# Where a pair mask is made in a graph-net and expert kernel: moved from the expert block to the first row stage

## The reference

```python
x = x + L0_gnn(layernorm(x), src, dst, edge_attr_20, edge_weight, edge_attr_4, ...)   # message passing
x = x + L0_ffn(layernorm(x), gamma, beta, Wd, splines, Wu, scale)                    # one of 64 experts a row
x = x + L1_gnn(layernorm(x), edge_index, node_vec1, ...)                             # 4 blocks of attention + MLP
x = x + L1_ffn(layernorm(x), w_gate, w_up, w_down)                                   # gated feed-forward
# attention of L1_gnn, per head
scores = einsum('ehd,ehd->eh', q[src], k[dst])
attn = exp(scores - smax[src]) / segment_sum(exp(...), src)
out = segment_sum(attn[:, :, None] * v[dst], src)
```

## Time and profile before

| what | value |
|---|---|
| median of 3 runs | 2948.11 us |
| the profiled execution's own time | 2946.58 us |
| its span, first to last instruction | 2944.9 us |
| mean granted TensorE clock | 0.933 |
| busy: PE, PEld, DVE, ACT, POOL | 86%, 74%, 64%, 47%, 40% |
| moved by DMA | 220.43 MB |

### The profile page before, as it was taken

One profiled execution on the slowest core, in us unless ns is written; L12 is line 12 of the kernel. 1 busy time (PEld: TensorE's weight loads), 2 busy tenths in 40 slices (PEclk: granted clock), 3 DMA queues, 4 the chain that ended last, 5 costly groups with the idle time before them and its releaser, 6 DMA issues. The chain is left out here.

```text
span 2944.9 us, 38864 instructions
## 1 busy us (share of the span) xinstructions
PE 2521.8 (86%) x13585; PEld 2166.0 (74%) x13585; DVE 1889.2 (64%) x3545; ACT 1376.1 (47%) x2744; POOL 1183.7 (40%) x914
## 2 busy tenths in 40 slices
PE   3899999635756279999998998989989989998999
PEld 3687887534646267897786887878977878877997
DVE  2799999562653455677636777546777367777862
ACT  1566565421234344565435665435654356654431
POOL 2788888783773201235102234012251023273420
PEclk9999999857867689999999999999999999999999
DMA  7444444128539821101212111211011121021101
GB/s 246 89 89 80 84 80 91 7 36 241 156 72 279 226 70 52 35 18 55 66 34 72 33 31 55 70 53 35 18 53 64 39 68 37 21 88 48 53 13 35
DMA packets 171993, 220.43 MB, mean 75 GB/s; under 512 B 111698, under 2 KB 120333, under 8 KB 164372
## 3 DMA queue, kind: packets, MB, share of 16 engines
q1 hardware_dynamic: 80561, 171.84, 20.0%
q0 software_dynamic: 91232, 46.02, 8.1%
HBM read 177.10 MB, written 40.15 MB: 74 GB/s over the span
## 5 line engine op out<-in xcount | busy, mean ns | idle before, releaser
L2124 POOL TENSOR_SCALAR prob<-prob,rden,linked 125x1250 f32<-125x1250 f32 x160 | 224.0, 1400 | 920.1 <-DVE rden L2091 920.1
L580 POOL DMA_INDIRECT pairs<-late_cnt,late_idx x160 | 354.4, 2215 | 112.2 <-DMA pairs<-late_cnt,late_idx 61.7
L2042 ACT CAST prob_high<-ps 125x375 fp32r<-125x375 f32 (+1 forms) x480 | 231.3, 503 | 267.4 <-PE ps L2004 267.1
L2083 DVE CUSTOM_DVE_ANT_0 prob<-ps,mask 125x1250 f32<-125x1250 f32 x160 | 233.1, 1457 | 125.7 <-PE ps L1980 119.1
L2096 DVE TENSOR_TENSOR prob_low<-ps,prob_high 125x375 fp32r<-125x375 f32 (+1 forms) x480 | 270.0, 586 | 46.7 <-ACT prob_high L2042 46.7
L339 POOL DMA_INDIRECT Hg<-h_rows,dsti x160 | 231.0, 1444 | 118.6 <-issue 97.1
L1993 PE MATMUL ps<-ident,prob 125*125 125x125 f32 x1600 | 252.3, 273 | 17.3 <-POOL prob L2124 10.7
L1993 PEld LDWEIGHTS ps<-ident,prob 125*125 125x125 f32 x1600 | 232.3, 187 | 29.8 <-POOL prob L2124 22.9
L539 PE MATMUL ps<-onehot,mhi 125*128 125x512 f32 (+1 forms) x960 | 245.7, 364 | 6.0 <-DVE onehot L427 5.2
L539 PE MATMUL ps<-onehot,mlo 125*128 125x512 f32 (+1 forms) x960 | 238.8, 357 | 0.0
L2034 ACT ACTIVATE prob<-prob,top 125x1250 f32<-125x1250 f32 x160 | 214.6, 1341 | 42.1 <-DVE top L2083 33.8
(11 more groups left out here) (411 smaller groups left out, 6019.8 us busy)
## 6 DMA issues: line engine op xcount, KB each, us to landing
mask<-mask_d SPq DMA_DIRECT2D x40, 546.9 KB
sg_wd<-L_ffn_Wd SPq DMA_DIRECT2D x32, 512.0 KB
w_ring<-L_ffn_Wd SPq DMA_DIRECT2D x16, 1024.0 KB, 7.4
w_ring<-L_ffn_Wu SPq DMA_DIRECT2D x16, 1024.0 KB, 9.9
pairs<-zeros POOLq DMA_DIRECT2D x18, 625.0 KB, 26.2
keyrow<-keys_d SPq DMA_DIRECT2D x40, 244.1 KB
kept<-g_d SPq DMA_DIRECT2D x40, 224.0 KB
g_d<-kept SPq DMA_DIRECT2D x30, 224.0 KB
```

What stands on the lines that cost most here:

```text
L580: nc.gpsimd.indirect_dma_start(pairs[a][:, :], bass.IndirectOffsetOnAxis(T.E.late_idx[:, c:c + 1], 0), T.E.late_cnt[:, c:c + 1], None, com ...
L2042: s.copy(M.pt[0][:, n % 3, 0:w], T.ps[0:P, 3 + n % 4, 0:w]).then_inc(high, 1)
L2083: v.tensor_tensor_reduce(M.prob[:, r, :], S(u)[0:P, 0:N], M.mask[:, it % MASKS, :], 1.0, 3.0e38, ALU.add, ALU.min, M.top[:, r:r + 1]).then ...
L2124: nc.gpsimd.tensor_scalar(M.prob[:, r, :], M.prob[:, r, :], M.rden[:, r:r + 1], T.linked[:, it:it + 1], ALU.mult, ALU.mult).then_inc(norme ...
```

## The change

- `LATE` has two parts only: 14 additions in `node_update` and 78 in `experts`. `expert_norm` and `route` have none.
- The ring of weights has 8 groups in place of 5. `route` loads five groups of experts ahead (3 to 7), and the nine over blocks are loaded by `experts`' SP after the scattered rows `xs`.
- `experts` makes no mask: the loads, the VectorE and ACT operations and the stores are gone there. POOL waits for all additions and gathers.
- The spills of `x_d` and `g_d` are issued by SP in the first row stage. The additions' results are loaded there through four pairs of buffers (`pair_c`, `pair_m`), which lie in the place of `v`; the summing (`count`) and the two comparisons (`cover`) are VectorE's after given units, the logarithm ACT's, the subtraction POOL's, loads and stores SP's. The load of a tile into a used buffer waits for the store of that buffer's mask.
- `wk` is loaded at the start of this stage. ACT writes `k_high` only after the spills have landed (the places overlap), and `v` waits for the stores from the buffers that it overwrites.
- The loop over three layers is written out.

```diff
-LATE = (EARLY_ADDS, EARLY_ADDS + 14, EARLY_ADDS + 24, EARLY_ADDS + 34, ET)
+LATE = (EARLY_ADDS, EARLY_ADDS + 14, ET)
...
-WG, RG = 4, 5
+WG, RG = 4, 8
...  expert_norm and route, POOL
-                    late_adds(pool, nc, T, pairs, 1)
-                    late_adds(pool, nc, T, pairs, 2)
...  route, SP; in experts behind the loads of xs
-                    sp.wait_ge(over_ready, 1)
-                    for g in range(OVERS):
-                        load_over(sp, A, R, g)
+                    for g in range(OVERS):
+                        load_over(sp, A, R, g)
...  experts, SP
-                    for t in range(NT - 2, NT):
-                        sp.wait_ge(l_ready, t + 1)
-                        wide(sp, mask_d[t * P:(t + 1) * P, :], pl[t % 2], mask_last)
-                    sp.wait_ge(added, NT)
-                    wide(sp, x_d.rearrange("(t p) d -> p t d", p=P), T.X, T.spilled)
-                    sp.wait_ge(rows_made, NT)
-                    wide(sp, g_d.rearrange("(t p) d -> p t d", p=P), first, T.spilled)
...  experts, POOL
-                    late_adds(pool, nc, T, pairs, 3)
+                    late_adds(pool, nc, T, pairs, 1)
                     for s in T.pair_added:
                         pool.wait_ge(s, ET * 8)
-                    for t in range(NT):   # loads of the counts, stores of the mask
...
+                    gather()
...  experts, ACT and DVE: logarithm, and the five operations a tile, are gone
...
+COUNT_AT = (6, 6, 7, 8, 9, 10, 12, 14, 16, 18)
+COVER_AT = (6, 7, 8, 9, 10, 11, 13, 15, 17, 19)
+LN_AT = (7, 8, 9, 10, 11, 12, 14, 16, 18, 20)
+MASK_SET = (0, 1, 2, 3, 0, 1, 2, 3, 1, 3)
+MASK_TURN = tuple(MASK_SET[:t].count(MASK_SET[t]) for t in range(NT))
...  rows_stage, SP
+                def load_pairs(t):
+                    k = MASK_SET[t]
+                    if MASK_TURN[t] >= 1:
+                        sp.wait_ge(mask_out[k], 32 * MASK_TURN[t])
+                    wide(sp, M.pair_c[k][:], counts[0][t * P:(t + 1) * P, :], pair_in[k])
+                    wide(sp, M.pair_m[k][:], counts[1][t * P:(t + 1) * P, :], pair_in[k])
+                def store_mask(t):
+                    sp.wait_ge(mask_made, t + 1)
+                    wide(sp, mask_d[t * P:(t + 1) * P, :], M.pair_c[MASK_SET[t]][:], mask_out[MASK_SET[t]])
...
+                if masks:
+                    load_pairs(0)
+                    load_pairs(1)
+                    wide(sp, x_d.rearrange("(t p) d -> p t d", p=P), T.X, T.spilled)
+                    wide(sp, g_d.rearrange("(t p) d -> p t d", p=P), M.first, T.spilled)
+                    sp.wait_ge(T.spilled, 64)
+                    load_pairs(2)
+                    load_pairs(3)
+                    store_mask(0)
+                    store_mask(1)
+                    load_pairs(4)
+                    store_mask(2)
+                    load_pairs(5)
+                    store_mask(3)
+                    load_pairs(6)
                 late(sp, cw_ready, cw_next, made, a_in, unit_made, v_in)
+                if masks:
+                    load_pairs(7)
+                    store_mask(4)
+                    store_mask(5)
+                    load_pairs(8)
+                    store_mask(6)
+                    store_mask(7)
+                    load_pairs(9)
+                    store_mask(8)
+                    store_mask(9)
+                    for k in range(4):
+                        sp.wait_ge(mask_out[k], 32 * MASK_SET.count(k))
...  rows_stage, POOL, behind the splits
+                    for t in range(NT):
+                        c, m = M.pair_c[MASK_SET[t]], M.pair_m[MASK_SET[t]]
+                        pool.wait_ge(empty, t + 1)
+                        pool.wait_ge(logd, t + 1)
+                        nc.gpsimd.tensor_tensor(c[:], m[:], c[:], ALU.subtract).then_inc(mask_made, 1)
...  rows_stage, ACT
+                        if n == 12 and source == "first":
+                            act.wait_ge(T.spilled, 64)
+                def logarithm(t):
+                    act.wait_ge(floor, t + 1)
+                    s.activation(M.pair_c[MASK_SET[t]][:], M.pair_c[MASK_SET[t]][:], ACT.Ln).then_inc(logd, 1)
...                  after take(n): logarithm(t) where n == LN_AT[t]
...  rows_stage, DVE
+                def count(t):
+                    k = MASK_SET[t]
+                    dve.wait_ge(pair_in[k], 64 * (MASK_TURN[t] + 1))
+                    v.tensor_tensor_reduce(M.pair_c[k][:], M.pair_c[k][:], M.pair_m[k][:], 1.0, 0.0, ALU.add, ALU.max,
+                                           M.pair_top[:, t:t + 1]).then_inc(summed_up, 1)
+                def cover(t):
+                    k = MASK_SET[t]
+                    dve.wait_ge(summed_up, t + 1)
+                    v.tensor_scalar(M.pair_m[k][:], M.pair_c[k][:], 0.5, BIG, ALU.is_lt, ALU.mult).then_inc(empty, 1)
+                    v.tensor_scalar(M.pair_c[k][:], M.pair_c[k][:], 1.0, None, ALU.max).then_inc(floor, 1)
                 for n in range(6, len(order)):
                     finish(n)
+                    for t in range(NT) if masks else ():
+                        if n == COUNT_AT[t]:
+                            count(t)
+                        if n == COVER_AT[t]:
+                            cover(t)
...  qkv_loads: for the first stage wk stands in loads, not in late
...
-        with nc.Fori(0, 3) as L:
+        for L in range(3):
```

More of the change, by code:

```diff
@@ L704 @@
 WIDTH = SLOTS + WIN
-WG, RG = 4, 5
-LN0, LNSTEP, LNS = 12, 8, 8
+WG, RG = 4, 8
 OVERS = -(-NOVER // WG)
@@ L1017, in experts @@
         tables = A["L0_ffn_splines"].rearrange("e k g h -> e (k g h)")
-        pc = sb("pm_c", [P, 2, N]); pm = sb("pm_m", [P, 2, N]); plog = sb("pm_l", [P, 2, N])
-        pl = (plog[:, 0, :], plog[:, 1, :])
-        top = sb("pm_top", [P, NT])
-        counts = [a[0:N * N, :].rearrange("(n m) a -> n (m a)", m=N) for a in pairs]
         rows = xs[:].rearrange("p t d -> p (t d)")[0:P]
@@ L1298, in _ @@
                                ).then_inc(y_copied, 1)
-                        if b >= LN0 and (b - LN0) % LNSTEP == 0 and (b - LN0) // LNSTEP < LNS:
-                            logarithm((b - LN0) // LNSTEP)
                     for t in range(NS_T):
@@ L1303, in _ @@
                         s.copy(ysb[:, t, :], T.ps[:, 4 + t % 4, :]).then_inc(yc_act, 1)
-                    for t in range(LNS, NT):
-                        logarithm(t)
                     for t in range(NT + 1):
@@ L1539, in __init__, with rows_stage @@
         self.top = at("top", 153280, [P, RING])
+        self.pair_c = [at(f"pair_c{s}", 154240 + 10048 * s + 1536 * (s // 2), [P, N]) for s in range(4)]
+        self.pair_m = [at(f"pair_m{s}", 159264 + 10048 * s + 1536 * (s // 2), [P, N]) for s in range(4)]
+        self.pair_top = at("pair_top", 153472, [P, NT])
         self.den = at("den", 153344, [P, RING]); self.rden = at("rden", 153408, [P, RING])
-def rows_stage(nc, T, M, source, sink, g_d, x_d, loads, late, bias, bqk, bvo, last=False):
+COUNT_AT = (6, 6, 7, 8, 9, 10, 12, 14, 16, 18)
[3 more added lines that the diff above has]
+MASK_TURN = tuple(MASK_SET[:t].count(MASK_SET[t]) for t in range(NT))
+def rows_stage(nc, T, M, source, sink, g_d, x_d, loads, late, bias, bqk, bvo, last=False, pairs=None, mask_d=None):
     NCH = len(PARTS)
@@ L1565, in rows_stage @@
         g = (lambda t: M.kept[t][:]) if pe_source else (lambda t: M.first[:, t, :])
+        masks = pairs is not None
+        if masks:
+            counts = [a[0:N * N, :].rearrange("(n m) a -> n (m a)", m=N) for a in pairs]
         def units():
@@ L2149, in loads @@
                 sp.dma_start(bqk[:, 1, :], one(par("bk", L))).then_inc(b_in, 16)
+                if first:
+                    sp.dma_start(flat(M.raw_a), one(par("wk", L))).then_inc(a_in, 16)
             def late(sp, cw_ready, cw_next, made, a_in, unit_made, v_in):
```

76 lines of the change are left out of this document (29 added, 47 removed).

## The result

| what | before | after |
|---|---|---|
| median | 2948.74 us (4 runs) | 2898.26 us (4 runs, 2892.73 to 2904.57) |
| the profiled execution's own time | 2946.58 us | 2904.57 us |
| its span | 2944.9 us | 2902.8 us |
| mean granted clock | 0.933 | 0.939 |
| busy: PE, PEld, DVE, ACT, POOL | 86%, 74%, 64%, 47%, 40% | 87%, 75%, 65%, 47%, 41% |

A forecast was written before the change was run, and what follows sets the result against it. PE was taken as busy almost throughout, except in slices 8 to 15, where alone a mask change can gain. Terms: -86.3 before the row stage, +38 in it, -7.2 for the loop; -55.5 from 2946.6 gives 2891 us, range 2862 to 2922.

The forecast's parts named there:

- expert_norm: Stage `expert_norm`: without ten additions POOL starts sooner and ACT ends the stage; gain 9 us, bounds 8 and 12.
- route: Stage `route`: five scatters begin sooner and the stage takes 41 instead of 56.6 us; gain 15.6, bounds 10 and 19.
- Down and look-up: Those phases of `experts`: over blocks ahead of the spline tables cost 1 us, bounds 0 and 4; longer ring saves nothing.
- Up phase until the gather: In `experts`: waits at logarithms go; stores at +79, additions at +81, a near tie; gain 51.7 us, bounds 44 and 54.
- rival B: End of `experts`: additions at 4.5 us delay the gather, 2992 us, chance 0.07; mild form at 3.5, 2914 us, 0.10.
- Gather until the row stage: End of `experts`: spills no longer end the stage and the gather meets no mask traffic; gain 11 us, bounds 8 and 13.
- First row stage: Mask work moved there waits on transfers through four buffer pairs; 38 us longer, bounds 23 and 55.
- The port's 4 us: First row stage: the port VectorE and POOL share costs 4 us of VectorE's chain between +50 and +66.
- The loop: Layers written out: two turns, each 3.6 us of PE's wait for its first score; gain 7.2 us, bounds 0 and 8.
- A: First row stage hides the mask, a store and load together taking some 7 us: +5, 2858 us; chance 0.08.
- C: First row stage: the port in full, each of ten 3.3 us subtractions on PE's path, 33 us, 2920 us; chance 0.10.
- D: First row stage: transfers as slow as in the old stage, the upper bound of 55 us, 2908 us; chance 0.12.

The follow-up runs named there:

- the experiment: The changed kernel without POOL's ten subtractions in the first row stage, the store waiting for logarithm and comparison instead: row stage 159.2 us, time 2888.7 us.
- a cheaper mask in a better order: The changed kernel with one VectorE operation replacing comparison, maximum and subtraction, five and three buffers, transfers and sums reordered: row stage 123.8 us, 2857.84 us, ratio 0.9715.
- the run without reloads: The changed kernel with mask tiles 4 to 9 computed on what the buffers hold, without loads, zeros stored early: row stage 142.5 us, time 2869.63 us.
- additions spread: The changed kernel with eight of its 78 additions moved ahead, three to the start of `expert_norm`, five to that of `route`: 2893.74 us, ratio 0.985.

## Why the forecast held, and where it was off

*expert_norm.* -9.9 for -9. The mechanism is as told, down to the port: beside POOL's 13.18 us two VectorE operations took 3.49 us together and a third 1.75, where each takes 0.74 alone: 3.0 us, which is the 12 less the 9.

*route.* -17.5 for -15.6: the scatter ends it, as told, and landed in at most 6.5 us where 8.6 were taken.

*Down and look-up.* +2.3 for +1. The late tables were met (PE waits 3.58 us at 699.88). One sentence does not hold in the trace: "the longer ring saves nothing that I can see". With the over blocks behind `xs`, the ring of five makes PE wait 11.5 us; the forecast judged the ring by the trace of before, where the over blocks had been loaded in `route`. In the time the ring is worth 5 us by the medians, and these are not clear of noise.

*Up phase until the gather.* -41.9 for -51.7, the first of the two mis-sized terms. No logarithm holds PE; its 68 us came out, and so did the stores' +79 where they could be seen (79.7, 79.0 and 78.4 in the three traces in which the stores clearly decide). The additions: 28 were left when the phase began, not 26. 13 were issued in its first 47 us, as forecast (4 and 9); the other 15, from 886.12 to 924.30, came every 2.7 us where 13 at 2.4 were forecast. Two more and 0.3 us each are the 10 us. That is this execution's: in the nine traces the gather began 80.7 to 91.4 us behind the start, and the forecast's +81 is the lower end. The 78 additions took 3.3 us each, between the forecast's 3.2 and the 3.5 of rival B's mild form.

*Gather until the row stage.* -15.1 for -11, beyond its bound of 13. The DMA engines were busy 0.36 of this stretch, 0.76 before; what the 4 us more are made of is not shown.

*First row stage.* +51.5 for +38, the second mis-sized term, inside its bounds of 23 to 55. The kind of chain was right, its timing only up to tile 5. In us behind the stage's start, forecast and then measured: sum of tile 4 at 66 and 67.2; of tile 5 at 72 to 74 and 75.7; of tile 7 at 84 to 88 and 100.8; of tile 8 at 98 and 111.7; of tile 9 at 109 and 122.7; end of the last k unit at 119 and 133.9. All of the miss but a microsecond or two is there at tile 7. The forecast named `late`'s wait on its own transfers and gave it next to no time. SP stood 12.8 us in it until the conditioning weights had landed, and issued tile 7's load at +91.9. A tile was also slower than the 7 us taken: 7.7 to 10.3 us from its first issue to the start of its sum. SP's issue of the conditioning weights and of tile 7's load, and VectorE's sums of tiles 7 and 9:

```profile
1030.42 0.89 SPq L2183 DMA_DIRECT2D cw<-L_gnn_cond  x3
1047.63 0.32 SPq L142 DMA_DIRECT2D pair_c<-pairs  x1
1056.50 1.46 DVE L1890 CUSTOM_DVE_ANT_0 pair_c<-pair_c,pair_m 125x1250 f32<-125x1250 f32 x1 [12.54 <-DMA pair_m<-pairs]
1078.43 1.46 DVE L1890 CUSTOM_DVE_ANT_0 pair_c<-pair_c,pair_m 125x1250 f32<-125x1250 f32 x1 [7.14 <-DMA pair_m<-pairs]
```

The run with tile 7's load first fits this: its sum came at +88.9, near the forecast's time; but the wait stayed in the queue, tile 8 came at +112.3, and the stage kept its length. No run takes away this wait alone, so its price is read from the traces and not measured by itself. PE's 11.9 us more of busy time come from its lower clock behind each stall, and the forecast counted the lower level for one unit only. But most of them lie ahead of a further wait for a tile and lengthen nothing. On the path they count behind the last tile: the last three units took 9.0 us, 6.2 in before, and the forecast had 2 of these 2.8. The port's 4 us were 7 by the experiment.

*The loop.* -14.7 in this comparison for -7.2, and the 14.7 are not the loop's. The runs on the kernel before put writing it out at a gain of at most 6 us. The turn's gap is there in PE's rows, but the term took a difference between waits for a gain in time: in the changed kernel the two turns' waits are 9.6 us longer with the loop, and the stretch is 0.6 us longer. The Trainium skill ("Runtime: NRT & Kernel Launch", "Instruction fetch mechanics") says that a taken branch whose target is not in the fetched pages must fetch it first. The rows agree in that there is a gap (9.67 against 4.74 us), though no run shows that it is a fetch, and the time does not show it.

*The total.* It held in part by luck. The two mis-sized terms are 23.3 us, and 7.5 of the 10 that came back are the long stretch of one execution of before. Without the row behind the first row stage the profiled pair gives -27.4 for a forecast of -48.3; the medians give -41 to -50, and the profiled execution of after was the slowest of its four.

*Rivals.* A (+5 in the row stage) is refuted by the stalls; a cheaper mask in a better order nears it, +9. B in its strong form is refuted, its mild form is half right. C is refuted: 7 us, not 33. D, "transfers as slow as in the old stage", with 9.7 us for a load and 7 for a store, gave +55 and was near in both: loads took 7.7 to 10.3 us, and the two stores that a load waited for were done 9.6 and 6.1 us behind their first issue. Beside them stood SP's wait, to which D gave no time of its own.

## What to carry to other kernels

When work is moved under another stage, follow the queue that brings its data and give every wait in it a time. A wait in the middle of an in-order queue belongs to the queue: here a wait of 12.8 us for 0.2 MB of other weights, to which the forecast gave next to no time, stands where nearly the whole miss of the row stage arose. Moving one item ahead of it moved the stall to the next item. The versions without the stall order all transfers by need and put each consumer behind its transfer's arrival. A lower clock behind a stall shows in busy time (11.9 us here), and costs only where no further wait follows. And before a difference between two profiles is given to an edit, undo that edit: 14 us of the comparison here were not the loop's.

## What the runs showed of the hardware

- A `TENSOR_SCALAR` of 125x1250 floats on VectorE takes 0.81 us, and 3.4 to 3.5 when it begins just behind the start of POOL's subtraction of two such arrays; four 128x512 subtractions took 7.8 instead of 2.5. The sum of two arrays with a maximum (1.45 us) took 2.63 and 2.96 us in after, in the two cases where it began during a subtraction, and kept its length in the run without reloads, where none began during one.
- Turning a loop costs PE 9.4 to 9.7 us before its first matmul instead of 4.7, in the same kernel, and the kernel's time does not show it (2898.35 and 2895.35 us, both 0.9864 of before).
- The same program's gather began 80.7 and 90.8 us behind the up phase in two executions, on two chips. Additions by indirect DMA come every 2.3 us when nothing holds them; in the up phase of after they wait up to 5.3 us more for the one before the last, and in `route` with additions spread 9.8.
